# Two set-up jobs of the first slot given to GpSimd, and the third projection moved two items later

## What is computed

```python
xn = layernorm(x)
out = x + attention(xn) + experts(xn)
# attention: 16 heads of 8, causal softmax, projections Wq, Wk, Wv, Wo with biases
# experts: logits = xn @ gate_w.T over 8 experts, softmax over the best two,
#          out = sum of xn @ We[e], weighted, over these two
```

## Time and profile before

| what | value |
| --- | --- |
| median of 3 runs | 509.58 us (509.15 to 509.74) |
| the profiled execution, its own time | 508.7 us |
| its span, first to last instruction | 506.9 us |
| busy: PE, PEld, DVE, ACT, POOL | 93%, 72%, 84%, 78%, 68% of the span |
| mean granted TensorE clock | 0.989 |

### The profile page before, as it was taken

How to read it: one execution, slowest core, us unless ns; L and a number is a source line. 1 busy time by engine, 2 the same in 40 slices (tenths; PEclk the granted TensorE clock), 3 DMA queues, 4 the chain that set the end, 5 groups by cost and what they waited for, 6 DMA issues and landing times.

```text
span 506.9 us, 15266 instructions
## 1 busy us (share of the span) xinstructions
PE 470.8 (93%) x5250; PEld 367.4 (72%) x5250; DVE 424.0 (84%) x1111; ACT 396.4 (78%) x1062; POOL 347.1 (68%) x563
## 2 busy tenths in 40 slices
PE   2448799999999999999999999999999999999995
PEld 1326577787788787777878878778878888777753
DVE  4998669888989889888898988988889998888821
ACT  3655668888888888888888888888888888887773
POOL 7363737877777877777777777787777777755443
PEclk9999979999999999999999999999999999999998
DMA  4674745546556665654655666555556666651000
GB/s 124 170 168 97 192 128 133 143 125 166 139 133 152 157 161 135 160 143 114 160 149 136 155 162 157 146 140 149 139 127 155 147 153 157 150 135 32 14 14 22
DMA packets 64273, 67.66 MB, mean 133 GB/s; under 512 B 6828, under 2 KB 59180, under 8 KB 59484
## 3 DMA queue, kind: packets, MB, share of 16 engines
q1 hardware_dynamic: 64196, 66.68, 53.0%
HBM read 44.90 MB, written 21.23 MB: 130 GB/s over the span
## 4 chain that ended last, share of the span: by engine, by line
PE 84%; DMA 4%; DVE 3%; ACT 2%; issue 2%; SPq 2%; POOL 1%; POOLq 0%; DVEq 0%; ACTq 0%
PE m L852 21%; PE oT_ps L918 17%; PE scoreT_ps L895 12%; PE score_ps L877 11%; PE score_ps L872 5%; PE scoreT_ps L899 5%; PE m L960 3%; PE m L1003 3%; PE m L1021 3%; DMA qstack<-mT 2%; PE m L933 2%; PE m L1028 1%; DMA scratch<-parts 1%; PE m L969 1%; DVE qstack L720 1%
## 5 line engine op out<-in xcount | busy, mean ns | idle before, releaser
L636 DVE TENSOR_REDUCE negmax<-score_ps 128x2 f32<-128x512 f32 (+1 forms) x384 | 249.7, 677 | 40.9 <-PE score_ps L877 36.5
L510 ACT ACTIVATE probs<-scoreT_ps 128x512 f32<-128x512 f32 x384 | 216.9, 603 | 67.5 <-PE scoreT_ps L895 47.1
L406 POOL TENSOR_TENSOR fours<-lower,upper 128x512 f32<-128x512 f32 x64 | 81.7, 1277 | 51.7 <-ACT upper L560 51.5
L852 PE MATMUL m<-we_hl,xnT_hl 128*128 128x512 f32 x384 | 113.3, 417 | 0.0
L877 PE MATMUL score_ps<-kstack,qstack 123*128 123x256 bf16 x512 | 100.8, 279 | 5.8 <-DVE negmax L636 5.5
L895 PE MATMUL scoreT_ps<-qstack,kstack 123*128 123x256 bf16 x512 | 99.1, 276 | 5.3 <-DMA qstack<-mT 4.5
L918 PE MATMUL oT_ps<-probs,vaug 128*32 128x256 f32 (+1 forms) x2048 | 98.0, 332 | 0.2 <-ACT probs L510 0.2
L560 ACT ACTIVATE upper<-m,weight 128x128 f32<-128x128 f32 x256 | 73.1, 375 | 9.3 <-PE m L852 9.3
L918 PEld LDWEIGHTS oT_ps<-probs,vaug 128*32 128x32 f32 x2048 | 57.8, 110 | 30.1 <-issue 1.7
L852 PEld LDWEIGHTS m<-we_hl,xnT_hl 128*128 128x128 f32 x384 | 65.4, 191 | 9.1
L373 POOL TENSOR_TENSOR parts<-rest,parts 128x256 bf16<-128x256 f32 x60 | 40.1, 690 | 31.7 <-ACT parts L539 31.7
(11 more groups left out here) (83 smaller groups left out, 653.9 us busy)
## 6 DMA issues: line engine op xcount, KB each, us to landing
kstack<-scratch SPq DMA_DIRECT2D x93, 192.0 KB
scratch<-parts SPq DMA_DIRECT2D x64, 192.0 KB, 2.3
qstack<-scratch SPq DMA_DIRECT2D x62, 192.0 KB
qstack<-scratch SPq DMA_DIRECT2D x31, 256.0 KB
x_sb<-in_x SPq DMA_DIRECT2D x32, 128.0 KB, 2.3
scratch<-parts SPq DMA_DIRECT2D x32, 128.0 KB, 1.9
out<-out_sb SPq DMA_DIRECT2D x32, 128.0 KB, 3.3
qstack<-mT SPq DMA_DIRECT2D x64, 8.0 KB, 2.0
```

The costliest lines, as they stand in the source:

```text
L406: g.tensor_tensor(fours[:, :, q, :], lower[:, :, q, :], upper[:, :, q, :], ALU.add).then_inc(pool_sum, 1)
L510: a.activation(o, i, ACT.Exp, scale=SCALE).then_inc(act_exp, 1)
L636: v.tensor_reduce(o, score_ps[n % 2][:].rearrange("p (h k) -> p h k", h=w), axis=AX.X, op=ALU.max, negate=True).then_inc(dve_max, 1)
L852: ins = tn.matmul(o, l, r, start=first, stop=l is low)
```

## The change

Three things change, all in slot 0.

1. The experts' low half leaves VectorE (it stood behind `w_high` at item 5) and is made by GpSimd behind item 8, on the new semaphore `pool_weights`.
2. The mask rows of `qstack[3]` leave VectorE (item 8) and are copied by GpSimd right behind the low half, on the new semaphore `pool_stack`. GpSimd waits for each of the two before it goes on.
3. The projection of sequence 2, and all that follows it, comes two items later: `project` at item 3 (from 1), `part1` and `take_rest` at 4 (from 2), `part2` at 5 (from 3), `part3` at 6 (from 4). On GpSimd `part3` thereby passes behind the normalisation of sequence 3, on ScalarE `part1` and `part2` behind the gates' exponential.

```diff
--- before.py
+++ after.py
@@ -64,6 +64,9 @@
 B_STEPS = [-(2.0 ** (MASKED - FIRST_STEP + i * (MASKED - TINY))) for i in range(STEPS)]
 HIGH_BITS = 0xFFFFF000
 
+
+DVE_FILLS, ACT_FILLS, POOL_FILLS = [2, 4, 5, 5], [0, 0, 1, 2], [0, 0, 0, 1]
+
 GAP, TOTAL, GATES, SHARE, WEIGHT = range(1, 6)
 
 SUM_Q0, SUM_Q1, PAIRS, FOURS, RESULT = range(1, 6)
@@ -213,7 +216,7 @@
         act_stack, dve_stack, pool_fill, pool_zero, dve_zero, dve_weights, act_weights = sems(
             "act_stack", "dve_stack", "pool_fill", "pool_zero", "dve_zero", "dve_weights", "act_weights")
         dma_first = sem("dma_first")
-        pool_steps, ld_zero = sems("pool_steps", "ld_zero")
+        pool_steps, ld_zero, pool_weights, pool_stack = sems("pool_steps", "ld_zero", "pool_weights", "pool_stack")
         dma_x = sems(*(f"dma_x{b}" for b in range(NB)))
         dma_scratch_q, dma_scratch_k = sems("dma_scratch_q", "dma_scratch_k")
         dma_stack = sems(*(f"dma_stack{b}" for b in range(NB)))
@@ -293,9 +296,11 @@
                 sp.wait_ge(pe_score, upto(last, per=ITEMS))
                 stand_alone(sp, sp_passed)
                 if pre.n < NB:
-                    sp.wait_ge(dve_stack, 2 * (pre.n + 1) if pre.n < PRE else PRE + pre.n + 1)
+                    sp.wait_ge(dve_stack, DVE_FILLS[pre.n])
                     if pre.n >= PRE:
-                        sp.wait_ge(act_stack, pre.n + 1 - PRE)
+                        sp.wait_ge(act_stack, ACT_FILLS[pre.n])
+                    if pre.n > PRE:
+                        sp.wait_ge(pool_stack, POOL_FILLS[pre.n])
                     sp.wait_ge(ld_zero, 16 * NB)
                 rows = scratch[pre.buf].rearrange("a (d h) t -> (a d) h t", h=H)
                 qs, ks = qstack[pre.buf], kstack[pre.buf]
@@ -448,7 +453,7 @@
                     if n == 3 and has(s, -2):
                         pool.wait_ge(pool_sum, upto(fin, per=RESULT, k=PAIRS))
                         g.tensor_tensor(mixed[:], pairs[:, 0], pairs[:, 1], ALU.add).then_inc(pool_sum, 1)
-                    if n == 4 and has(s, PRE):
+                    if n == (6 if s == 0 else 4) and has(s, PRE):
                         part3(t + PRE)
                     if n == 5 and has(s, -2):
                         pool.wait_ge(pool_sum, upto(fin, per=RESULT, k=FOURS))
@@ -465,6 +470,14 @@
                         gates(t, WEIGHT)
                     if n == 7 and has(s, -1):
                         sum_tile(t + (-1), 0)
+                    if s == 0 and n == 8:
+
+                        pool.wait_ge(dve_weights, 3)
+                        g.tensor_tensor(we_hl[:, 1], we_sb[:], w_high[:], ALU.subtract).then_inc(pool_weights, 1)
+                        pool.wait_ge(pool_weights, 1)
+                        g.tensor_copy(qstack[PRE + 1][HALF:P], q_steps[HALF:P].rearrange("p q t -> p (q t)").unsqueeze(1)
+                                      .to_broadcast([HALF, H, S])).then_inc(pool_stack, 1)
+                        pool.wait_ge(pool_stack, 1)
 
             g.memset(zeros[:], 0.0).then_inc(pool_const, 1)
             g.memset(minus_half[:], -0.5).then_inc(pool_const, 1)
@@ -538,9 +551,9 @@
                     act.wait_ge(dve_rest, upto(pre, per=2, k=c + 1))
                     a.copy(parts[:, c, 1, :], rest[:, c, :]).then_inc(act_part2, 1)
 
-            def fill_keys(b):
-
-                a.copy(kstack[b][HALF:P], k_steps[HALF:P].rearrange("p q t -> p (q t)").unsqueeze(1).to_broadcast(
+            def fill_rows(stack, steps):
+
+                a.copy(stack[HALF:P], steps[HALF:P].rearrange("p q t -> p (q t)").unsqueeze(1).to_broadcast(
                     [HALF, H, S])).then_inc(act_stack, 1)
 
             def copy_input(nxt):
@@ -570,7 +583,7 @@
                         act.wait_ge(pe_mT, upto(mix))
                         act.wait_ge(dma_max, upto(mix + (-1), per=MAX_PARTS, unit=16))
                         a.copy(mT[:, 0], m0[0:H, 0:S]).then_inc(act_mT, 1)
-                    if n == 2 and has(s, PRE):
+                    if n == (4 if s == 0 else 2) and has(s, PRE):
                         part1(t + PRE)
                     if n == 6 and has(s, -2):
                         act.wait_ge(pe_pv, upto(fin, per=NG))
@@ -585,14 +598,14 @@
                     f, k = behind(t, s, n)
                     if f:
                         take_exp(f, k)
-                    if n == 3 and has(s, PRE):
+                    if n == (5 if s == 0 else 3) and has(s, PRE):
                         part2(t + PRE)
                     if n == 3 and has(s, 0):
                         act.wait_ge(pool_gate, upto(t, per=WEIGHT, k=GAP))
                         act.wait_ge(pool_gate, upto(t + (-1), per=WEIGHT, k=GATES))
                         a.activation(numer[:, :, 1], gap[:], ACT.Exp).then_inc(act_gate, 1)
                     if s == 0 and n == 5:
-                        fill_keys(PRE + 1)
+                        fill_rows(kstack[PRE + 1], k_steps)
                     if s == 0 and n == 7:
                         act.wait_ge(dve_weights, 3)
                         a.copy(we_hl[:, 0], w_high[:]).then_inc(act_weights, 1)
@@ -617,7 +630,7 @@
                     part1(Seq(0, k))
                     part2(Seq(0, k))
             act.wait_ge(pool_steps, MASK_SIGNALS)
-            fill_keys(PRE)
+            fill_rows(kstack[PRE], k_steps)
             over_slots(slot)
 
 
@@ -749,10 +762,6 @@
                         dve.wait_ge(ld_we, 16)
                         dve.wait_ge(act_weights, 1)
                         high_half(we_sb[:], w_high[:]).then_inc(dve_weights, 1)
-                        dve.wait_ge(dve_weights, 3)
-                        low_half(we_sb[:], w_high[:], we_hl[:, 1]).then_inc(dve_weights, 1)
-                    if s == 0 and n == 8:
-                        fill_stack(qstack[PRE + 1], q_steps)
                     if n == 4 and has(s, 0):
                         best_numbers(t)
                     if n == 5 and has(s, 0):
@@ -968,7 +977,7 @@
                         for q in range(QT):
                             ins = tn.transpose(m0[0:H, q * P:(q + 1) * P], negmax[mix.buf][:, q], ident[:])
                         ins.then_inc(pe_mT, 1)
-                    if n == 1 and has(s, PRE):
+                    if n == (3 if s == 0 else 1) and has(s, PRE):
                         pe.wait_ge(act_upper, upto(fin, per=2))
                         project(pre)
                     if n == 3 and has(s, -2):
@@ -976,7 +985,7 @@
                         values(fin, 1)
                     if n == 4 and has(s, -1):
                         if s == 1:
-                            pe.wait_ge(dve_weights, 4)
+                            pe.wait_ge(pool_weights, 1)
                             pe.wait_ge(act_weights, 2)
                         if has(s, 0):
                             pe.wait_ge(act_v, upto(t))
```

## The result

The changed kernel took **506.69 us** (median of 12 runs, 504.6 to 508.8), and the kernel before 508.98 us (median of 12 runs, 508.5 to 510.53): a ratio of 0.9948, 95% interval 0.9934 to 0.9962, or 1.9 to 3.4 us gained. The profiled execution took 507.75 us, with a span of 505.8 us at a mean granted clock of 0.992.

A forecast was written before the change was run, and what follows sets the result against it. Bound: VectorE's slot 0 and the chain on SyncE's list behind it, then TensorE after about 70 us. 1.09 + 1.14 + 1.26 - 0.3 - 0.1 = 3.1 us off 509.58 gives 506.5 us; range 504.8 to 509.0.

The forecast's parts named there:

- The projection: In slot 0, moving it two items later removes VectorE's wait before the third score item: 1.09 us gained.
- The low half: In slot 0, taking the experts' low half off VectorE gains 1.14 us.
- the fill: In slot 0, taking the fill of `qstack3` off VectorE gains 1.26 us, less 0.1 us allowed for gaps.
- `w_high`: On VectorE in slot 0, it loses between nothing and 0.67 us beside GpSimd's `part3`; 0.3 us taken.
- slot 1's first item: At slot 1's start, due at 35.3 us, it should find the stack of sequence 1 landed, with little to spare.
- Two of the signs: At the end of slot 0's chain: `mT` at SyncE near 39.5 us, and TensorE's hole ending near 60.8 us.
- A: Rival: GpSimd's copy takes its upper bound of 10.2 us; 509.0 us, or 507.5 at half that excess; chance 0.13.
- B: Rival: the parts of sequence 2 come too late, SyncE waits in slot 1; at 4 us late, 509.6 us; chance 0.09.
- C: Rival: VectorE's halving of sequence 3 waits for GpSimd's fill; 510.7 us, near 516 at the upper bound; chance 0.05.
- D: Rival: TensorE's idle hole shrinks and the clock may not fall there; up to 3.4 us more, 503 to 505; chance 0.05.
- After about 70 us nothing waits for anything but TensorE: Behind the last hole, 60 to 70 us, moving the start of TensorE's busy stretch moves the end by as much.

The follow-up runs named there:

- e5: The changed kernel with an added 512 KB store to a scratch tensor that nothing reads, behind slot 0's input load; one run, 506.88 us.
- e4: The changed kernel with the stack of sequence 1 loaded in two halves of eight heads; 505.94 us, 0.9922 of the kernel before.
- e3: The changed kernel with the projection put back, leaving GpSimd's two jobs alone; 507.1 us, 0.9943 of the kernel before.
- e2: The kernel before with the projection of sequence 2 alone moved; 508.67 us, 0.9983 of the kernel before.
- e1: The changed kernel again, nothing altered; 505.98 us, 0.9934 of the kernel before.
- e6: The kernel before again, nothing altered, for a second trace; one run, 507.96 us.
- e9: The changed kernel with the stack of sequence 1 loaded in two halves, once more; 507.27 us, 0.9935 of the kernel before.

## Why the prediction was right

Forecast and result agree (506.5 forecast; 506.69, in a range of 504.8 to 509.0), and the mechanism is the one forecast: VectorE gets through slot 0 earlier, and what hangs on SyncE's list follows. But two steps of the sum were off, on opposite sides, and the agreement to 0.2 us is luck in part: counted as a gain, 3.1 us were forecast and 2.3 measured, since the kernel before now read 508.98 us and not the 509.58 that the forecast started from.

**The terms on VectorE were all a little small.** The projection gave 1.30 us rather than 1.09: the third maximum begins 2.38 us after the first score instead of 3.68. In the trace that I read VectorE came late to the first score, being still at `bias_out`; where it does so again, with the first score before 22.6 us, the third maximum begins at 2.54 (e5) and 2.61 (e4), and the gain is 1.14 and 1.07, as forecast. The low half gave 1.25 (from `w_high` to `hit`, 31.52 to 33.38 before and 31.50 to 32.11 in e3; forecast 1.14), the fill 1.32 (34.16 to 39.07 before and 32.89 to 36.48 in e3; forecast 1.26 less 0.1 for gaps, but the last five maxima have none). Together 3.87, against 3.90 measured (3.7 in e4, 3.8 in e5).

**`w_high` lost nothing** (0.69 us, 0.68 before), where I took 0.3 off. Beside it stood the normalisation's `xn`, not `part3`, and it was `xn` that stretched: 2.25 us for the two in slot 0, 1.59 in slot 1; the second of them, on GpSimd:

```profile
31.08 1.46 POOL L368 TENSOR_SCALAR xn<-x_sb,mv,rstd 128x128 f32<-128x128 f32 x1
```

The Trainium skill (SBUF — State Buffer, § Who interferes with whom) would have the one that starts first run on and the other wait; `hit` at 0.66 us beside `part3` in e2 agrees with that, and this pair does not, by the starts in the trace: `xn` began at 31.08, 0.08 us ahead of `w_high`, and it was `xn` that took longer. The pair that I had weighed, `w_high` and `part3`, did not meet in the changed kernel.

**The step that failed** is "slot 1's first item, due at 38.4 - 3.1 = 35.3, should find it there, with little to spare". I had read the landing of one DMA in one execution (7.6 us) and taken it for what it would be with the change too. It was 7.0 to 8.5 in the four traces with the projection unmoved named above, and 9.5 to 11.3 in the five with it moved. The price is the distance from halving to `mT` beyond 3.51 us: 2.03 in after, 1.56 in e1, 1.25 in e5. So 3.9 became 1.9 to 2.5 us, where 3.1 was written. Two of the signs that I had named were missed by it: `mT` came to SyncE at 41.67, not near 39.5, and the hole ended at 62.83, not near 60.8, where 0.96 us of each miss is the later start of slot 0 in that trace. Had I asked what of the gain is lost if that landing is 2 or 3 us later, it would have been a rival with a sizeable chance, since the margin was nil by my own sum.

**The rivals.** A fell: the copy took 3.59 or 3.60 us in all eight traces that have it, below my lower end of 3.8 for it. The Trainium skill's price of about 6 us for the first call of a freshly loaded kernel (GPSIMD Engine Reference, § Instruction dispatch) is not in that row. B fell: 9.3 us lay between the last part's store and the load that reads it. C did not come about, but not by the test that I had in mind: the halving was done (36.13 to 36.55) before the copy began (36.96), in this trace as in the others. Beside GpSimd's other job, the low half, it took 0.42 us, and the five maxima ahead of it 0.69 each; what did stand beside the copy, the first two maxima of slot 1, took 1.29 us (1.28 before). My upper end for C was reckoned wrong, too: a fill that ends at 46.2 costs 10.2 - 3.1 = 7.1 us, which is 516.7 and not near 516. D is not the change's doing: in the stretch from 60 to 70 us the granted clock was 0.66 or 0.83 in all but two traces, with the change and without it; only e6, the kernel before, had 1.00 there, and e4 0.72.

**"After about 70 us nothing waits for anything but TensorE"** is true of the trace of before but for one wait of 0.26 us, and not of every execution. From slot 3 on most slots follow one another by 14.13 us, but in the fourteen traces the distance from slot 3's product with `wvg_sb` to the last one is between 394.95 and 397.67 us, with no order by kernel (395.25 and 397.67 are both the kernel before). In e1, for example, TensorE waits again in the middle of the program:

```profile
121.32 0.38 PE L904 MATMUL scoreT_ps<-qstack,kstack 123*128 123x256 bf16 x2 [0.73 <-DMA qstack<-mT]
```

Together with the clock behind the hole (from its end to slot 3's product: 7.98 us in e6 at 1.00, 9.53 to 9.60 in the five traces at 0.83, 9.86 to 10.77 in the seven at 0.66) this is a scatter of 2 to 3 us in one execution, as large as the gain. It is why a single span tells little here: e9 shows `mT` at 39.41 and a span of 506.8, e6 `mT` at 43.09 and a span of 506.2.

## What to carry to other kernels

Count each trace from an event of its own (here the first score) before comparing two: the engines' work then agrees to some hundredths of a microsecond, at worst 0.2 (12.58 to 12.80 in the table), and what is left is the DMAs' landing. When a chain is shortened, look at what its next stage also needs; a DMA that came "just in time" in one trace becomes the bound, and its landing has to be given a spread, not a value, and may move with the change itself. Of two moves, price the second with the first made: a neighbour on another engine can take back half of a move that is free once the first is there.

## What the runs showed of the hardware that was not expected

A copy of 64 x 4096 bfloat16 took GpSimd 3.60 us where VectorE needs 1.22, and the two maxima that VectorE ran beside it did not stretch (1.29 us, 1.28 before); a `hit` of 128 x 32 beside `part3` went from 0.18 to 0.66 us. Loading a stack in two halves brought the stack's first half in before slot 1 asks for it, although SyncE spends 2 to 3 us more on issuing the loads (the input load behind them goes out at 29.67 in e4 and 27.20 in after, and lands at 33.9 and 38.5). Between 25 and 33 us the queue moved 201 to 207 GB/s in the four traces with the projection unmoved and 154 to 183 in the five with it moved, its engines about as busy (0.88 and 0.87 in before and after); why the whole stack lands so much later was not tried by itself.
